# Second layer of a two-layer attention and experts kernel: the split moved from pair 30 to pair 26, two features of 32 moved from VectorE to ScalarE

## The reference

```python
# L1 attention, for each of 4 sequences of 512 tokens, A = 64
e      = relu(signed_sqrt(q[:, :, None, :] + k[:, None, :, :]))   # (i, j, A)
scores = einsum('bija,a->bij', e, Wphi)
ex     = exp(scores - max(scores))
part1  = einsum('bij,bjc->bic', ex, Vy)
Ew     = einsum('bij,bija->bia', ex, e)
part2  = Ew @ We_w.T + We_b * denom
attn   = (part1 + part2) / (denom + EPS)
# L1 experts: 8 experts for each token, weighted by the top 2 gates
y_e    = silu(((x@w1+b1) * (x@w2+b2)) @ wg + bg) @ w3 + b3
x      = x + attn + sum_e we * y_e
```

## Time and profile before

| | us |
|---|---|
| median of 3 runs (lowest, highest) | 1387.46 (1384.8, 1387.72) |
| the profiled execution's own time | 1383.03 |
| its span in the trace | 1381.3 |
| VectorE busy, whole span | 1212.5 |
| TensorE matmul busy, whole span | 1210.2 |
| ScalarE busy, whole span | 1135.1 |
| GpSimd busy, whole span | 888.8 |
| 31 us of the second layer (762 to 793): VectorE, ScalarE, TensorE, GpSimd busy | 28.95, 28.09, 28.03, 25.38 |
| TensorE's granted clock in that stretch | 1.00 |

### The profile page before, as it was taken

How to read it: one execution, slowest core, us unless ns; L and a number is a source line. 1 busy time by engine, 2 the same in 40 slices (tenths; PEclk the granted TensorE clock), 3 DMA queues, 4 the chain that set the end, 5 groups by cost and what they waited for, 6 DMA issues and landing times.

```text
span 1381.3 us, 21175 instructions
## 1 busy us (share of the span) xinstructions
PE 1210.2 (88%) x6185; PEld 575.5 (42%) x6185; DVE 1212.5 (88%) x3409; ACT 1135.1 (82%) x1292; POOL 888.8 (64%) x1294
## 2 busy tenths in 40 slices
PE   3899999998659999888999989899988889998886
PEld 2577667676422333333333333333333333333333
DVE  5777989896778899999999999989999998999997
ACT  1776888886369998999999899999989999998950
POOL 0764733332007888888888788888888888888820
PEclk9999999999769999999999999999999999999998
DMA  6001100000000001000000100000000000001001
GB/s 193 9 11 24 30 1 0 0 1 1 20 0 16 20 20 28 23 27 20 20 20 20 32 23 24 20 20 20 20 31 27 20 21 20 20 21 31 28 20 35
DMA packets 38843, 32.36 MB, mean 23 GB/s; under 512 B 6150, under 2 KB 35609, under 8 KB 38738
## 3 DMA queue, kind: packets, MB, share of 16 engines
q1 hardware_dynamic: 37714, 29.76, 7.4%
q0 software_dynamic: 1024, 1.35, 0.6%
HBM read 29.10 MB, written 2.75 MB: 23 GB/s over the span
## 4 chain that ended last, share of the span: by engine, by line
DVE 35%; PE 32%; issue 5%; ACT 1%; POOL 0%; POOLq 0%; DVEq 0%; ACTq 0%
DVE arena L1051 21%; PE ps L1331 10%; PE ps L1344 9%; DVE arena L1037 5%; PE ps L1388 4%; PE ps L1408 4%; DVE s L1083 3%; DVE x L1094 2%; PE ps L1380 2%; PE ps L1362 2%; DVE spread L1103 2%; DVE nmax L1043 1%; PE ps L1366 1%; ACT arena L1190 1%; DVE shift L1045 0%
## 5 line engine op out<-in xcount | busy, mean ns | idle before, releaser
L1051 DVE SCALAR_TENSOR_TENSOR arena<-arena,ps 128x512 f32<-128x512 f32 x1024 | 663.8, 677 | 69.8 <-PE ps L1344 68.5
L1190 ACT ACTIVATE arena<-arena,eps 128x4096 f32<-128x4096 f32 x128 | 474.2, 3709 | 6.0 <-ACT arena L1178 5.7
L1308 POOL TENSOR_SCALAR arena<-kT,negq 128x512 f32<-128x512 f32 x480 | 344.0, 723 | 170.8 <-DVE arena L1051 161.8
L1344 PE MATMUL ps<-spread,sel 128*128 128x512 f16 x1024 | 357.9, 386 | 101.1 <-DVE arena L1051 95.0
L1314 POOL TENSOR_SCALAR arena<-arena,q 128x512 f32<-128x512 f32 x480 | 348.0, 735 | 22.4
L1344 PEld LDWEIGHTS ps<-spread,sel 128*128 128x128 f16 x1024 | 91.9, 97 | 491.5 <-DVE arena L1051 376.0
L1331 PE MATMUL ps<-arena,phi_cols 128*32 128x512 f32 x2048 | 276.3, 614 | 7.7 <-ACT arena L1190 7.7
L1178 ACT ACTIVATE arena<-kT,q 128x512 f32<-128x512 f32 x330 | 217.1, 712 | 44.3 <-DVE arena L1051 44.3
L462 POOL TENSOR_SCALAR kT<-kT,region 128x512 f32<-128x512 f32 x128 | 88.8, 694 | 155.6 <-DVE region L587 155.0
L512 ACT ACTIVATE kT<-ps,region 128x512 f32<-128x512 f32 x128 | 88.0, 687 | 59.4 <-DVE region L582 57.9
L1395 PE MATMUL ps<-z,wge 128*128 128x512 f32 x256 | 130.8, 593 | 0.3 <-DVE z L1077 0.3
(11 more groups left out here) (196 smaller groups left out, 1714.9 us busy)
## 6 DMA issues: line engine op xcount, KB each, us to landing
wge<-in_e_wg SPq DMA_DIRECT2D x32, 256.0 KB, 2.7
w1e<-in_e_w SPq DMA_DIRECT2D x32, 128.0 KB, 2.1
w2e<-in_e_w SPq DMA_DIRECT2D x32, 128.0 KB, 2.1
w3e<-in_e_w SPq DMA_DIRECT2D x32, 128.0 KB, 2.1
region<-in_w SPq DMA_DIRECT2D x1, 2048.0 KB
out<-x SPq DMA_DIRECT2D x4, 256.0 KB, 2.8
region<-in_wqk SPq DMA_DIRECT2D x1, 512.0 KB, 4.7
region<-in_wv SPq DMA_DIRECT2D x1, 512.0 KB, 5.4
```

The source lines that it names most:

```text
L1051: dve.scalar_tensor_tensor(feat[:, j, k, :], feat[:, j, k, :], 1.0, psB[:, k % BANKS, :], ALU.mult, ALU.mult, accum_out=sums[:, j, gg, c:c ...
L1190: act.activation(grp, grp, ACT.Sqrt, bias=eps[:]).then_inc(e_ready, 2)
L1308: pool.tensor_scalar(feat[:, j, QUADS * gg + c, :], kT[:, b * N:(b + 1) * N], HUGE, negq[:, b % 2, at - b * N // 2:at - b * N // 2 + 1], A ...
L1344: pe.matmul(psB[:, k % BANKS, :], sel[:, gg, c, :], spread[:, j, :], start=True, stop=True).then_inc(bc_done, 1)
```

## The change

Two tables are edited. `ON_DVE` loses its entries for groups 0 and 3, so that VectorE makes 3 features of a block and ScalarE, which takes what is left, 13; GpSimd keeps 16. ScalarE's feature counts for the groups go from 1, 2, 1, 1, 2, 1, 1, 2 to 2, 2, 1, 2, 2, 1, 1, 2. `SPLIT_AT` goes from slot (7, 1), behind k=29, to (6, 1), behind k=25. All counts that the waits use are worked out from these tables.

```diff
@@ -941,7 +941,7 @@
     MB = TOK // BLK
     BB = N // BLK
     ON_POOL = [2, 2, 2, 2, 2, 2, 2, 2]
-    ON_DVE = [1, 0, 1, 1, 0, 1, 1, 0]
+    ON_DVE = [0, 0, 1, 0, 0, 1, 1, 0]
     ON_ACT = [QUADS - d - p for d, p in zip(ON_DVE, ON_POOL)]
@@ -1020,7 +1020,7 @@
-        SPLIT_AT, SILU_AT, LIFT_AT = (7, 1), ((7, 0), (7, 2)), 6
+        SPLIT_AT, SILU_AT, LIFT_AT = (6, 1), ((7, 0), (7, 2)), 6
         AHEAD_EXP = (1, 0)
```

## The result

| | before | after |
|---|---|---|
| median of 11 runs each | 1384.80 | 1389.18 |
| lowest, highest | 1380.01, 1387.97 | 1387.88, 1391.22 |
| ratio, 95% interval | | 1.0034, 1.0020 to 1.0048 |
| span of the profiled execution | 1381.3 | 1388.6 |
| period of a block in the steady part | 30.05 | 30.25 |

The kernel is slower by 0.34%, though VectorE, which was busiest, has 10.7 us less to do. The eight runs added since the forecast moved the median of before from 1387.46 to 1384.80.

What follows compares the result with a forecast made beforehand. TensorE was taken to set k=31 to k=14 of each block, VectorE the rest. Collisions +0.71 less 0.46 for the feature gave +0.25, over 30 blocks +7.5, on 1387.46: 1395.0, range 1378.5 to 1406.

Steps and rivals of the forecast that it cites:

- The two parts of a block: TensorE decides from k=31 to k=14, VectorE from k=14 to k=31; group 0's feature buys nothing, group 3's gains 0.46.
- The split releases nothing: Next block's first broadcast waits for k=30's bank however early the split is; the 1.7 us a block are no gain.
- First meeting: Behind k=25: GpSimd's second lift starts at 831.01, the split at 831.09, so the split is delayed 0.35.
- The tie: Behind k=26: VectorE's group 5 feature at 832.72 against GpSimd's 832.73; taken as first, at its normal 0.41.
- Rival 1: Tie at 832.72 goes to GpSimd, group 5's feature held 0.51 more: +0.57 to 0.59 a block, 1405.2; chance 0.25.
- Third meeting: Group 6's feature, VectorE at 836.89: GpSimd starts 0.16 ahead and holds until 837.23, delay 0.34.
- The term for a block: k=31 comes 0.71 later by collisions and 0.46 earlier by group 3's feature: +0.25 a block.
- the walk: Step-by-step start times of the new order at the block's end, from k=25 at 830.48 to k=31 at 837.62.
- The number of blocks: The +0.25 a block was taken over 30 blocks (m = 2 to 31), giving +7.5.
- The base: The 7.5 was put on the median of three, 1387.46, giving 1395.0.
- ScalarE gives back 0.12 or more in the naive case: Features alone: the root for groups 6 and 7 lacks slack, so the 0.46 gain loses 0.12 to 0.18 a block.

Runs made afterwards that it cites:

- changing one slot alone: VectorE makes group 1's feature in place of group 2's, against the kernel before, split still behind k=29: 1358.46, ratio 0.9813.
- the fill: Changed kernel with GpSimd's lift (s = tanh + 1) replaced by a memset of s to 1.0, which only writes: 1380.34, ratio 0.9968 to the kernel before.
- behind k=21: Kernel before with the split moved up behind k=21 (SPLIT_AT slot (5, 1)), features as before: 1401.55, ratio 1.0116.

## Where the prediction was right, and which step failed

The mechanism came out as it was written down. What failed is the last step, the sum's size: "+0.25" a block, "over 30 blocks +7.5", "put on that median". Measured were +0.20 a block, +4.2 over the parts of the trace that the change touches, +4.4 between the medians, and a median before of 1384.80 and not 1387.46. The forecast time lies 10.2 above that median, the measured one 4.4.

- **The two parts of a block.** Right. Group 3's feature, forecast at 0.46, was worth 0.43 alone; group 0's was worth 0.00 alone and 0.03 in the changed kernel.
- **The split releases nothing.** Right: 0.63 slower when moved alone.
- **First meeting.** Forecast: GpSimd's lift leads by 0.08, the split takes 0.35 more. The trace: 0.06 and 0.36.
- **The tie.** Forecast: VectorE 0.01 ahead, taken as a coin that falls its way. The trace: 0.02, and it fell its way in all steady blocks. Rival 1 did not occur. The prediction itself says that 0.01 is no lead, and its one row for VectorE was a lead of 0.04, so as far as the text goes its coming out was luck. The trace of before had a row that bears on it, which was not used: VectorE's feature at 430.10 takes 0.48 and GpSimd's instruction, shown 0.02 ahead of it at 430.08, takes 0.97. VectorE keeps its time there even when it is shown as second, so a tie is likelier to be VectorE's than a coin would say.

```profile
430.10 0.48 DVE L1037 TENSOR_SCALAR arena<-kT,q 128x512 f32<-128x512 f32 x1
```

```profile
430.08 0.97 POOL L1314 TENSOR_SCALAR arena<-arena,q 128x512 f32<-128x512 f32 x1
```

- **Third meeting.** Forecast: GpSimd leads by 0.16, 0.34 more. The trace: 0.20, 0.31 to 0.32.
- **The term for a block was too large.** The two meetings were forecast at 0.71 together with roundings and are worth 0.67 in the changed kernel's steps, 0.63 in the period of the split moved alone; less the feature, +0.25 was forecast and +0.20 measured. From the split's start to k=31 the walk had 6.53 (831.09 to 837.62) and the trace has 6.49 (805.80 to 812.29). For a difference of two sums of 0.7 and 0.5, a twentieth of a microsecond is a fifth of the result.
- **The number of blocks, and the ends of the loop.** 30 full periods were counted, and nothing for the loop's ends. At +0.20 the 30 periods would make 6.0. The time from the first to the last pair of exponentials is 933.65 before (402.48 to 1336.13) and 938.60 after (405.56 to 1344.16), 4.95 more: 28 periods of 0.20 make 5.6, the first is 0.45 longer, the last 0.26 shorter, and one block of before had 0.79 of a delay that the changed kernel's trace lacks. From there to the end the changed kernel is 0.74 shorter. That gives 4.2 in place of 6.0, which fits the 4.4 of the medians and is a larger miss than that of the term for a block. Why the ends behave so was not looked into.
- **The spans of the two profiles look like a hit and are none.** They differ by 7.3 (1381.3 and 1388.6), next to the forecast 7.5. But 3.1 of it lies ahead of the first pair of exponentials, in work that the edit does not touch: TensorE's 32 matmuls of the gate logits took 3.83 in the first profile and 6.83 in the second, at a granted clock from 358 to 362 of 0.87 and of 0.50, which is 1.2 GHz.

```profile
358.61 3.83 PE L901 MATMUL psL<-region,xnT 128*128 128x8 f32 x32
```

```profile
358.95 6.83 PE L901 MATMUL psL<-region,xnT 128*128 128x8 f32 x32
```

- **The base.** The 7.5 were put on a median of three. Eight more runs moved that median by -2.7, so that 1395.0 lies 5.8 above the measured 1389.18: 2.7 of it by the base and 3.1 by the size. Against the three runs that the text had, the measured time is up by only 1.7. Runs of the same kernel lie up to 8.0 apart (1380.01 to 1387.97); whether the 3 us of the matmuls above are a part of that is not shown, since only one run of it was profiled.
- **ScalarE gives back 0.12 or more in the naive case.** Wrong, though the forecast of the changed kernel did not use it. With the features alone it gave back nothing; I took 0.1 for the signal from the root's end, and the trace shows 0.05 from the end to the start of the products. Of the slack of 0.68, 0.63 was used.

## What to carry to other kernels

Before moving an instruction between engines, find in the timeline which engine sets each part of the loop: a feature was worth 0.43, 0.72 or nothing by its slot, and changing one slot alone gave 26 us. Then look at what the move does to its neighbours: where equal instructions show different durations (here 0.47 and 0.90, 0.74 and 1.10), look for another engine's instruction that started just before. An edit that leaves the count of work the same turned two of three "first" places into "second" ones. For a difference of some tenths of a per cent, work out the loop's ends and don't trust a base of three runs.

## What the runs showed of the hardware

Who starts first keeps its time, down to a lead of 0.02 for VectorE (807.43 against 807.45) and of 0.04 for GpSimd (1075.34 against 1075.38). Below that the shown starts do not tell: at 430.08 against 430.10 GpSimd is shown first and is the one that is held. Both sides have a hold that is shorter than the shown duration: 0.50 of a 0.69 GpSimd instruction, 0.43 of the 0.62 lift, 0.62 of the split's 0.74. A GpSimd instruction that only writes (the fill, 0.53) does not hold the split. The Trainium skill has that last rule in "SBUF — State Buffer", section "Who interferes with whom", for a VectorE instruction with two SBUF inputs, and the trace agrees. Being first is not free either: GpSimd lost 0.43 by coming second behind k=21, and VectorE then lost 0.30 and 0.38 at the two features behind it.
